# Exponential tables loaded by a one-column activation, the last down projection moved behind two score steps, and the score bank pairs exchanged

## The reference

```
hs = x @ sw1 + sb1;          shared = (silu(a) * b) @ sw2 + sb2
probs = softmax(x @ gate_w + gate_b);  cw = the two largest, zero elsewhere
hr = x @ rw1[e] + rb1[e];    routed = sum over e of cw[e] * ((silu(a) * b) @ rw2[e] + rb2[e])
```

## Time and profile before

| | |
|---|---|
| median of 3 runs | 1694.81 us |
| the profiled execution: its time, its span | 1692.39 us, 1690.6 us |
| TensorE matmul busy | 1426.2 us, 84% of the span, 15448 instructions |
| VectorE busy | 1116.9 us, 66% |
| ScalarE busy | 981.9 us, 58%, 1585 instructions |
| GpSimd busy | 319.2 us, 19% |
| mean granted TensorE clock | 0.954 of full speed |
| the chain that ended last, by engine | PE 18%, ACT 5%, DVE 5%, issue 2% (shares of the span) |

### The profile page before, as it was taken

How to read it: one execution, slowest core, us unless ns; L and a number is a source line. 1 busy time by engine, 2 the same in 40 slices (tenths; PEclk the granted TensorE clock), 3 DMA queues, 4 the chain that set the end, 5 groups by cost and what they waited for, 6 DMA issues and landing times. The chain is left out here.

```text
span 1690.6 us, 39028 instructions
## 1 busy us (share of the span) xinstructions
PE 1426.2 (84%) x15448; PEld 881.3 (52%) x15448; DVE 1116.9 (66%) x3235; ACT 981.9 (58%) x1585; POOL 319.2 (19%) x428
## 2 busy tenths in 40 slices
PE   1667798889898889889888888989889898989867
PEld 1445564655556465555546465555646555554433
DVE  5657676766767676776767677676767667646334
ACT  3154674765757575675747476574747656572632
POOL 3421121211212121111212111131212102020120
PEclk7588999999999999999999999999999999997988
DMA  5414213122130402212040312203040211010000
GB/s 91 82 23 52 56 19 57 17 43 37 24 55 9 70 10 42 31 34 46 14 65 9 52 22 43 37 20 59 9 66 14 38 30 34 3 30 4 13 7 7
DMA packets 79214, 58.05 MB, mean 34 GB/s; under 512 B 11004, under 2 KB 78902, under 8 KB 79030
## 3 DMA queue, kind: packets, MB, share of 16 engines
q1 hardware_dynamic: 76420, 53.96, 18.8%
q10 hardware_dynamic: 2610, 1.58, 0.7%
HBM read 11.57 MB, written 4.19 MB: 9 GB/s over the span
## 5 line engine op out<-in xcount | busy, mean ns | idle before, releaser
L969 DVE TENSOR_REDUCE chunkmax<-ps 128x3 f32<-128x384 f32 (+1 forms) x1024 | 507.5, 554 | 128.2 <-PE ps L1273 122.8
L690 ACT ACTIVATE probs<-ps 128x768 f32<-128x768 f32 (+1 forms) x512 | 404.4, 810 | 141.8 <-PE ps L1268 137.9
L1336 PE MATMUL ps<-zT,w 128*128 128x512 f32 x576 | 277.7, 600 | 2.5 <-ACT silu_a L707 2.5
L707 ACT ACTIVATE silu_a<-ps,b 128x512 f32<-128x512 f32 x144 | 98.8, 686 | 200.3 <-PE ps L1336 200.1
L1253 PE MATMUL ps<-k_op,q_op 48*128 48x256 bf16 x512 | 147.7, 290 | 61.4 <-DVE chunkmax L969 44.0
L1235 PE MATMUL ps<-q_op,k_op 51*128 51x256 bf16 x512 | 142.5, 278 | 43.4 <-ACT probs L690 16.3
L1090 DVE SCALAR_TENSOR_TENSOR h_open<-ps,b,silu_a 128x512 f32<-128x512 f32 x128 | 95.9, 749 | 120.7 <-PE ps L1336 116.3
L1336 PEld LDWEIGHTS ps<-zT,w 128*128 128x128 f32 x576 | 105.0, 191 | 111.0 <-issue 97.3
L1362 PE MATMUL ps<-hT,w 128*128 128x512 f32 x288 | 149.1, 598 | 12.3 <-DVE hT L1096 12.3
L1253 PE MATMUL ps<-xk_op,xq_op 51*128 51x256 bf16 x512 | 144.2, 283 | 4.5 <-DVE chunkmax L969 4.1
L1265 PE MATMUL ps<-mask_q_lo,ident_lo 64*128 64x256 bf16 x512 | 146.3, 288 | 0.0
(11 more groups left out here) (235 smaller groups left out, 3426.5 us busy)
## 6 DMA issues: line engine op xcount, KB each, us to landing
q_op<-q_parts SPq DMA_DIRECT2D x192, 64.0 KB
xq_op<-xq_parts SPq DMA_DIRECT2D x192, 64.0 KB
k_op<-k_parts SPq DMA_DIRECT2D x168, 64.0 KB
x_tm<-in_L_attn_hidden_states SPq DMA_DIRECT2D x16, 256.0 KB, 5.9
x_keep<-in_L_attn_hidden_states SPq DMA_DIRECT2D x16, 256.0 KB, 6.1
out<-o_tm SPq DMA_DIRECT2D x16, 256.0 KB, 2.3
k_op<-k_parts ACTq DMA_DIRECT2D x24, 64.0 KB
w<-in_L_ffn_rw SPq DMA_DIRECT2D x1, 1024.0 KB
```

Of the source, the lines that this page charges most:

```text
L690: act.activation(probs[:, four % 2, 2 * pair:2 * pair + 2, 0:T + a.seen], ps[:, 2 * (g % 2):2 * (g % 2) + 2, 0:T + a.seen], ACT.Exp).then_ ...
L969: dve.tensor_reduce(chunkmax[:, b, at, :], ps[:, MAX_BANK[n], 0:3 * a.seen].rearrange("p (c n) -> p c n", c=3), AX.X, ALU.max).then_inc(a. ...
L1336: pe.matmul(ps[:, bank, :], w, src[:], start=True, stop=True).then_inc(sig.sem, 1)
```

## The change

- `exp_table()` is one activation with the Exp function from a 128x1 tile into a 128x1 tile that nothing reads. ScalarE issues it at the end of its body, behind the last silu, and in front of the first exponential of phase 2, behind the normalised sum.
- Even g now use banks 2 and 3, odd g banks 0 and 1, in `score_step` and in `exps`.
- The last `down` and its wait on `h_sb` move from the end of the body into the next body's phase 1, between step 1 and step 2. The wait on `h_sb` at the start of the body goes.
- The wait on `n_end.out` moves from ahead of phase 2 to between its steps 1 and 2.
- VectorE takes the first two maxima of phase 1 ahead of `expert_sum`.

```diff
@@ ScalarE
-                                   ps[:, 2 * (g % 2):2 * (g % 2) + 2, 0:T + a.seen], ACT.Exp).then_inc(a.exp.sem, 1)
+                                   ps[:, 2 * (1 - g % 2):2 * (1 - g % 2) + 2, 0:T + a.seen], ACT.Exp).then_inc(a.exp.sem, 1)
...
+            def exp_table():
+
+                act.activation(table_slot[:], half_neg[:, 0:1], ACT.Exp)
...
                 if exists(i - 1):
+                    exp_table()
                     exps(ca, i - 1, used, 0, 4)
...
                 if exists(i - 2):
                     experts(i - 2, 4, NE + 1)
+                if exists(i + 1):
+                    exp_table()
@@ VectorE
+                if exists(i - 1):
+                    maxima(ca, i - 1, 0, 2)
                 if exists(i - 3):
                     expert_sum(i - 3)
                 if exists(i - 1):
-                    maxima(ca, i - 1, 0, 2 * H)
+                    maxima(ca, i - 1, 2, 2 * H)
@@ TensorE
-                    bank = ps[:, 2 * (g % 2) + hh, :]
+                    bank = ps[:, 2 * (1 - g % 2) + hh, :]
...
                     for step in range(4 * four, 4 * four + 4):
+                        if step == 2:
+                            free_01()
                         score_step(a, j, par, step, other, jo, paro, step, free_4, free_5)
...
+                def last_down():
+
+                    if exists(k - 1):
+                        pe.wait_ge(*h_sb.before(k))
+                        down(k - 1, NE)
+
+                def free_sum_tokens():
+
+                    if exists(i - 3):
+                        pe.wait_ge(*n_end.out.done(i - 3))
...
-                if exists(k - 1):
-                    pe.wait_ge(*h_sb.before(k))
...
-                    attention_phase(sa, i, par, ca, i - 1, 1 - par, free_sum, free_gate)
+                    attention_phase(sa, i, par, ca, i - 1, 1 - par, free_sum, free_gate, last_down)
...
-                if exists(i - 3):
-                    pe.wait_ge(*n_end.out.done(i - 3))
                 if i > 0:
-                    attention_phase(ca, i - 1, 1 - par, sa, i + 1, 1 - par, free_self_output, free_mlp)
+                    attention_phase(ca, i - 1, 1 - par, sa, i + 1, 1 - par, free_self_output, free_mlp, free_sum_tokens)
...
                 if exists(k):
                     experts(k, 4, NE + 1)
-                    down(k, NE)
```

More of the change, by code:

```diff
@@ L140, in sandwich_kernel @@
         wait_slot = sb("wait_slot", [128, 1])
+        table_slot = sb("table_slot", [128, 1])
         maxT = sb("maxT", [3 * H, NT], BF16)
@@ L1292, in value_group, with attention_phase @@
                 last.then_inc(a.pv.sem, 1)
-            def attention_phase(a, j, par, other, jo, paro, free_4, free_5):
+            def attention_phase(a, j, par, other, jo, paro, free_4, free_5, free_01):
                 if exists(j):
@@ L1406, in body @@
                     pe.wait_ge(*ca.qhi.done(i - 1))
-                if exists(k - 1):
-                    pe.wait_ge(*h_sb.before(k))
                 if i == 0:
-                    attention_phase(sa, 0, 0, sa, 1, 1, free_sum, free_gate)
+                    attention_phase(sa, 0, 0, sa, 1, 1, free_sum, free_gate, last_down)
                 else:
-                    attention_phase(sa, i, par, ca, i - 1, 1 - par, free_sum, free_gate)
+                    attention_phase(sa, i, par, ca, i - 1, 1 - par, free_sum, free_gate, last_down)
                 if exists(i):
```

## The result

| | before | changed |
|---|---|---|
| median | 1694.01 us (1692.2 to 1696.81, 4 runs) | 1663.3 us (1662.49 to 1663.69, 4 runs) |
| profiled execution: time, span | 1692.39, 1690.6 us | 1663.36, 1661.6 us |
| mean granted TensorE clock | 0.954 | 0.952 |

The ratio of the runs, changed to before, is 0.9816, with a 95% interval of 0.9802 to 0.983. The forecast was 1663.4 us.

The account below looks back on a forecast made before the run. No single engine was taken to bound the kernel, but a chain of waits passing between engines at phase starts. 28.6 + 1.3 + 0.5 + 1.0 = 31.4 us off 1692.4 gave 1661.0, plus 2.4: 1663.4 us; range 1656 to 1678.

Parts of the forecast that it names:

- Steps 0 and 1 in the gap: Phase 1 start: the steps take 0.69 us, fill TensorE's idle 0.81 us, and leave the last down projection on time.
- The table load hidden in phase 1: Phase 1 start: load (1.28 us) and small activation end before the scores arrive; exponential 0 starts 3.1 us earlier.
- two queues together give the gain: Phase 1: two separate queues give 2.2 us a body, between bounds of 1.3 (load only) and 3.1 (exponential 0's shift).
- Maximum 2 sets exponential 2: Phase 1: maximum 2, behind the copy of the sum, is late next; exponential 2 starts 2.2 us earlier.
- 2.2 us a body: Phase 1 gain in each of 13 bodies (3 to 15): 28.6 us.
- The shift is whole: Phase 1 behind step 10: TensorE is the pace, so the rest of the body keeps the full 2.2 us.
- The rival of VectorE's hold: Phase 1: VectorE, two maxima behind, costs 1.0 of the 2.2 us; gain 18.4 us, 1676 us, chance 0.16.
- The other rivals: Shift given back, 1692 us, 0.05; TensorE clock falls, 1708 us, 0.03; load put back, 1665 us, shares the forecast's chance.
- Phase 2: Hidden table load gains 0 in the 13 bodies with phase 2 queries, 1.3 us in body 15, 0.5 in body 16.
- Body 16, phase 1: No keys there, VectorE runs maxima without pause; two moved ahead of the copy gain 1.0 us.
- The drain: Rule against part of the forecast: 1380 ns on top of each table load; bodies 15 and 16 lose 0.9, sum 28.7 us.

Follow-up runs that it names:

- e1: The changed kernel without both one-column activations, so the table loads go back in front of each phase's first exponential: 1669.32 us, ratio 0.9844 to 0.9881.
- e2: The kernel before with the two one-column activations added and nothing else: 1674.84 us, ratio 0.9873 to 0.9903.
- e3: The changed kernel with VectorE's order of before, the copy of the sum ahead of all maxima: 1675.95 us, ratio 0.9881 to 0.991.
- e4: The changed kernel with phase 2 as before: no one-column activation there, the wait for the sum's norm ahead of step 0: 1666.19 us.
- e9: The kernel before with the bank pairs exchanged and nothing else: 1695.10 us, ratio 0.9991 to 1.001.
- e5: The changed kernel run once more, unedited, beside later edits: 1664.27 us.

## Why the prediction was right

- **Steps 0 and 1 in the gap.** Taken: the down projection isn't late. Measured: 0.09 us late behind hT. The 0.69 us of the sum go from the start of step 0 to the start of step 2. To the end of step 1's last matmul (767.30) it is 0.84 us, just more than the gap of 0.81.
- **The table load hidden in phase 1.** As said; the row behind the last silu shows it. That two queues together give the gain was right too: e1 keeps 1.90 of 2.11 us without hiding the load, though hiding it alone (e2) brings 1.23.
- **Maximum 2 sets exponential 2.** Shown by e3, which puts maximum 2 two reductions later and loses 0.94 us a body. By its sum it was 0.98, with 0.49 for each; eight reductions take 3.85 us and six 2.91, so one more takes 0.47. e2 agrees: it too has maximum 2 two reductions later, and gets 1.23 of 2.11.
- **2.2 us a body.** Measured 2.11. Exponential 2 starts 3.06 us behind hT (at 770.33: 769.39 and 1.75, less its own 0.81), where 2.93 were counted. Some half of the 0.13 missing is the late down projection (maximum 2 at 1.89 against 1.83). The rest is the way from maximum 2 to exponential 2, 1.17 us against the 1.10 of the sum. 13 x 2.11 = 27.4 against 28.6 us.
- **The shift is whole.** Right: behind step 10, where TensorE still waits for exponential 3, its one wait of over 0.2 us for a maximum in the rest of phase 1 of body 8 is 0.22 us, as before the change. The rival of VectorE's hold fell for that reason. Its number, 1676 us, is what e3 has, but e3 has another cause: all maxima stand behind the copy. The other rivals fell too: bodies 2 to 15 keep 27.5 of 28.6 us, so little was given back; the mean granted clock is 0.952 against 0.954; and no load of the exponential's table waits for TensorE.
- **Phase 2.** Zero in bodies 3 to 14, shown by e4's body. Body 15 gave 1.27 for 1.3 and body 16 0.54 for 0.5 at the exponentials.
- **Body 16, phase 1.** From the first GELU of body 15 to that of body 16 the profiled executions differ by 1.99 us (83.48 and 81.49), where 1.3 and 1.0 were counted. Neither is kept whole, and the traces tell them apart. From the first GELU to the first silu of body 15, behind phase 2, it is 32.83 us before and 31.73 after: 1.10 of the 1.27. From that silu to the first GELU of body 16, with phase 1 between, it is 50.63 to 50.85 us in the four kernels in which VectorE copies first (before, e2, e3, e9), and 49.76 to 49.85 in four that take two maxima first (changed, e1, e4, e5): 0.89 of the 1.0 between before and changed.
- **The start of the kernel.** The sum had nothing here, and the profiled execution of the changed kernel had its first GELU 1.0 us later (224.73 against 223.73). That need not be the change's: over the profiled executions this mark lies between 223.72 and 227.54 us, the last of them in e9, which has the waits of before. Between the profiled executions of before and e9 it makes 3.8 of 4.9 us.
- **The time.** The profiled execution was forecast at 1661.0 us and took 1663.36: 1.1 us are missing in the bodies, 1.0 went at the start, and the rest in bodies 15 and 16. The forecast then added 2.4 us, by which the median of before lay above its profiled execution; the changed kernel's median is no higher than its own. So the two errors of 2.4 us cancelled, and the 0.1 us between forecast and median is luck. The body's 2.11 against 2.2 is the fair measure.
- **The drain.** The Trainium skill (ScalarE: Activation LUTs, "What ACT_TABLE_LOAD costs") adds 1380 ns of drain to a table load. The changed kernel doesn't show it either: the small activation starts 0.01 us behind the load (765.39, 1.28, 766.68), and exponential 0 of body 15 comes 1.27 us earlier, where that rule left nothing.

## What to carry to other kernels

A function table load in front of a wait-bound activation can be drawn ahead by a one-column activation of the same function, behind the last use of the old table. What it brings depends on which queue is late next: here 1.23 us a body alone, 0.21 on top of the moves, and nothing in phase 2 of the regular bodies. When a phase starts on several engines at once, work out the second operation that each waits for, not the first: the order of one copy and two reductions was worth nearly half of the change. Small groups of instructions of a side task fit into a paced loop where the whole group doesn't.

## What the runs showed of the hardware

- Bodies differ within one execution by 0.1 to 0.3 us: before, 96.76 to 97.09. Most of it is a short stretch at half clock. In the traces of before and changed each such stretch from body 2 to body 14 starts 0.4 to 2.0 us behind TensorE's wait of some 1.6 us for the first maximum of phase 2. The tables-only kernel (e2) has none there, nearly all of its bodies at 95.53 to 95.59 and the higher mean granted clock, 0.958. Two bodies are long without one: the distance from body 10 to body 11 is 94.93 us in the changed kernel and 95.82 in e2, and why stays open. So is which bodies get a stretch.
- A table load takes 1.28 us in every trace here, and the activation behind it starts 0.01 us later, but for one near the end of each that waits for VectorE (in the changed kernel 1.33 us, ahead of 1622.17).
